# Reordering the seams of a four-deep software pipeline: row statistics, output norm, turned maxima and the residual

## What is computed

```python
def block(x, c):                                   # layers L0, L1, L2, each with its own weights
    s1, c1, g1, s2, c2, g2 = split(silu(c) @ w_mod + b_mod, 6)
    y = layernorm(x) * (1 + c1) + s1
    q, k, v = split(y @ w_qkv + b_qkv, 3)          # 16 heads of 18
    q, k = norm_per_head(q), norm_per_head(k)      # L0: RMS-like, L1: none, L2: centred, with gain and shift
    o = softmax(q @ k.T * 18 ** -0.5) @ v          # per head, 256 x 256
    x = x + g1 * (o @ w_o + b_o)
    y = layernorm(x) * (1 + c2) + s2
    return x + g2 * (gelu(y @ w1 + b1) @ w2 + b2)  # 288 -> 1152 -> 288
U = qr(P).Q                                        # 288 x 64
x = x + ((x @ U) @ expm(A(c)) - x @ U) @ U.T       # after the third block
```

## Time and profile before

| | |
|---|---|
| time, median of 3 runs (lowest to highest) | 5283.6 us (5277.15 to 5285.2) |
| time of the profiled execution | 5279.16 us |
| its span, first to last instruction | 5277.4 us |
| mean granted TensorE clock | 0.942 |
| PE busy | 4467.7 us (85%) |
| DVE busy | 3683.8 us (70%) |
| ACT busy | 2297.4 us (44%) |
| POOL busy | 1110.9 us (21%) |

### The profile page before, as it was taken

How to read it: one execution, slowest core, us unless ns; L and a number is a source line. 1 busy time by engine, 2 the same in 40 slices (tenths; PEclk the granted TensorE clock), 3 DMA queues, 4 the chain that set the end, 5 groups by cost and what they waited for, 6 DMA issues and landing times. The chain is left out here.

```text
span 5277.4 us, 125546 instructions
## 1 busy us (share of the span) xinstructions
PE 4467.7 (85%) x46073; PEld 3701.5 (70%) x46073; DVE 3683.8 (70%) x7723; ACT 2297.4 (44%) x3828; POOL 1110.9 (21%) x2044
## 2 busy tenths in 40 slices
PE   6654888888888886899999999976988989899888
PEld 4543677777777775777777777765777777777776
DVE  5665788777877774666666666656777777777774
ACT  0112445454444543444444444434444444444443
POOL 1001222222222212222222222212122121212121
PEclk7576999999999997999999999997999999999999
DMA  3001010010100001010000100011000000000000
GB/s 69 19 0 47 26 27 27 23 27 21 27 27 24 26 21 55 26 27 25 23 27 27 27 27 27 25 42 31 24 26 19 26 24 21 24 23 26 19 24 17
DMA packets 122230, 141.59 MB, mean 27 GB/s; under 512 B 14446, under 2 KB 117780, under 8 KB 122112
## 3 DMA queue, kind: packets, MB, share of 16 engines
q1 hardware_dynamic: 121968, 139.75, 9.7%
q10 hardware_dynamic: 144, 0.22, 0.0%
HBM read 110.87 MB, written 29.06 MB: 27 GB/s over the span
## 5 line engine op out<-in xcount | busy, mean ns | idle before, releaser
L627 ACT ACTIVATE pT<-S 128x1024 f32<-128x1024 f32 x768 | 745.2, 1022 | 467.5 <-PE S L1134 463.1
L863 DVE TENSOR_REDUCE mx<-S 128x4 f32<-128x1024 f32 x768 | 919.1, 1215 | 26.9 <-PE S L1105 20.0
L575 ACT ACTIVATE hf<-M 128x512 f32<-128x512 f32 (+1 forms) x480 | 266.8, 556 | 927.1 <-PE M L1185 842.7
L922 DVE TENSOR_TENSOR xbo<-M,gM 128x288 f32<-128x288 f32 x192 | 87.8, 457 | 784.1 <-PE M L1224 784.1
L1134 PE MATMUL S<-qT,kT 32*128 32x256 f32 x9216 | 432.2, 298 | 159.3 <-ACT nmT L614 83.7
L504 POOL TENSOR_SCALAR hh<-hf 128x512 fp32r<-128x512 f32 (+1 forms) x480 | 282.7, 589 | 1192.1 <-ACT hf L575 1173.5
L1134 PEld LDWEIGHTS S<-qT,kT 32*128 32x128 f32 x9216 | 336.3, 187 | 240.2 <-ACT pT L627 108.1
L1144 PE MATMUL A<-pT,V 128*32 128x256 f32 x6144 | 415.9, 389 | 19.6 <-ACT pT L627 19.6
L1185 PE MATMUL M<-xh,w_hi 128*128 128x256 f32 x1728 | 388.0, 304 | 4.6 <-POOL xh L480 3.3
L1185 PE MATMUL M<-xl,w_hi 128*128 128x256 f32 x1728 | 347.6, 284 | 40.4 <-DVE xm L786 40.4
L1105 PE MATMUL S<-kT,qT 32*128 32x256 f32 x3072 | 351.2, 337 | 30.9 <-DVE mx L863 24.0
(11 more groups left out here) (229 smaller groups left out, 10190.6 us busy)
## 6 DMA issues: line engine op xcount, KB each, us to landing
mid<-xbo SPq DMA_DIRECT2D x64, 288.0 KB, 3.2
xld<-mid SPq DMA_DIRECT2D x64, 288.0 KB, 3.0
xa<-mid SPq DMA_DIRECT2D x64, 288.0 KB, 3.5
gA<-gates SPq DMA_DIRECT2D x96, 144.0 KB, 3.3
gM<-gates SPq DMA_DIRECT2D x96, 144.0 KB, 3.0
xld<-in_x_dram SPq DMA_DIRECT2D x32, 288.0 KB, 3.5
xa<-in_x_dram SPq DMA_DIRECT2D x32, 288.0 KB, 3.5
out_dram<-xbo SPq DMA_DIRECT2D x32, 288.0 KB, 2.2
```

Source lines behind the costliest of these rows:

```text
L575: act.activation(hf[:, f % 2, 0:c], MBANK[f % 2][:, 0:c], ACT.Gelu if rot else ACT.Gelu_apprx_tanh).then_inc(s["m_hf"], 1)
L627: act.activation(pT[:, g % 2, 2 * h:2 * h + 2, :], S[:, 2 * h:2 * h + 2, :], ACT.Exp, scale=float(HD) ** -0.5).then_inc(s["a_ex"], 1)
L863: dve.tensor_reduce(mx[:, p, :, :], S[:, r:r + 2, :].rearrange("p a (t k) -> p a t k", t=NT), AX.X, ALU.max).then_inc(s["a_mx"], 1)
```

## The change

No operation is added or removed; steps change their places, and one changes its bank.

- DVE: the first half of `M_x2(d)` goes behind both layer norms' statistics and normalisations; `A_heads_norm(p)` goes ahead of the second half of `M_x2(d)`; `R_x3` (third layer) and `A_out(a)` go ahead of `A_lo(p)`; `A_olo` and `M_hl(m, 0)` go ahead of `A_max(p, 1)`; `A_xl(nxt)` goes from ahead of `A_oraw` to a place between `A_max(p, 2)` and `A_x1(a)`.
- PE: `A_turn_max` goes into the previous slot, between `A_qkv(nxt, 4)` and the rest of `down0`, and writes to the fourth score bank, so that it no longer waits for a_qkvd; `A_pv(a, 0)` has that wait now. `down1` is cut at 16 and 22 of its 27 matmuls (first and second layer; before at 9 and 18) and at 16 (third layer; before at 14). `A_turn_n(a)` goes ahead of the scores 0 and 1.
- ACT: `A_shift` goes between the copies of `A_qkv` 4 and 5, in the previous slot.
- POOL: `M_residual` goes behind the first two `M_hh`.

The core of the diff (lines with # name the engine's function):

```diff
 # POOL, slot
-                            M_residual(m)
                             if rot:
                                 M_xh(m)
-                            for f in range(5):
+                            M_hh(m, 0)
+                            M_hh(m, 1)
+                            M_residual(m)
+                            for f in range(2, 5):
                                 M_hh(m, f)
...
 # ACT, A_shift
-                        act.activation(nmT[:, :], ABANK[0][:, 0:T], ACT.Identity).then_inc(s["a_nmc"], 1)
+                        act.activation(nmT[:, :], S[:, 3, 0:T], ACT.Identity).then_inc(s["a_nmc"], 1)
...
 # ACT, slot
-                            A_shift(a)
                             for i in range(2 * QUADS):
...
                             A_qkv(nxt, 4)
+                        if p is not None:
+                            A_shift(p)
+                        if nxt is not None:
                             A_qkv(nxt, 5)
...
 # DVE, slot
-                        if d is not None:
-                            M_x2(d, 0)
                         if m is not None:
                             M_stats(m)
...
                             M_norm(m)
+                        if d is not None:
+                            M_x2(d, 0)
                         if p is not None and eps is not None:
                             A_heads_rstd(p)
+                            A_heads_norm(p, None)
                         if d is not None:
                             M_x2(d, 1)
-                        if p is not None and eps is not None:
-                            A_heads_norm(p, None)
-                        if nxt is not None:
-                            A_xl(nxt)
                         if a is not None:
                             A_oraw(a, 0)
                             A_oraw(a, 1)
+                        if d is not None and rot:
+                            R_x3(d)
                         if m is not None and not rot:
                             M_xl(m)
+                        if a is not None:
+                            A_out(a)
                         if p is not None:
                             A_lo(p, 0)
                             A_lo(p, 1)
-                        if d is not None and rot:
-                            R_x3(d)
-                        if a is not None:
-                            A_out(a)
-                        if p is not None:
                             A_max(p, 0)
                         if m is not None and rot:
                             M_xl(m)
-                        if p is not None:
-                            A_max(p, 1)
-                        if m is not None and not rot:
-                            M_hl(m, 0)
                         if a is not None:
                             A_olo(a)
                         if m is not None:
-                            if rot:
-                                M_hl(m, 0)
+                            M_hl(m, 0)
+                        if p is not None:
+                            A_max(p, 1)
+                        if m is not None:
                             M_hl(m, 1)
                         if p is not None:
                             A_max(p, 2)
+                        if nxt is not None:
+                            A_xl(nxt)
                         if a is not None:
                             A_x1(a)
...
 # PE
-                    def A_turn_max(n, p):
-
-                        if p is not None:
-                            wait(pe, "a_qkvd", p, 6)
-                        wait(pe, "a_prd", n, 0)
+                    def A_turn_max(n):
+
                         wait(pe, "a_nm", n, 1)
                         for t in range(NT):
-                            op = pe.transpose(ABANK[0][:, t * P:(t + 1) * P], nm4[:, t, :, :].rearrange("p r h -> p (r h)"), ident[:, :])
+                            op = pe.transpose(S[:, 3, t * P:(t + 1) * P], nm4[:, t, :, :].rearrange("p r h -> p (r h)"), ident[:, :])
...
-                    def A_pv(n, g):
+                    def A_pv(n, p, g):
...
                         if g == 0:
                             wait(pe, "a_v", n, 2)
+                            wait(pe, "a_prd", n, 0)
+                            if p is not None:
+                                wait(pe, "a_qkvd", p, 6)
...
 # PE, slot
-                            A_turn_max(a, p)
                             A_scoresT(a, 0)
-                            down1(0, 14 if rot else 9)
+                            down1(0, 16)
                             A_scoresT(a, 1)
-                            A_pv(a, 0)
+                            A_pv(a, p, 0)
                             if rot:
-                                down1(14, 27)
+                                down1(16, 27)
...
                             if not rot:
-                                down1(9, 18)
+                                down1(16, 22)
...
                             if not rot:
-                                down1(18, 27)
+                                down1(22, 27)
...
+                        if a is not None:
+                            A_turn_n(a)
                         score(0)
                         score(1)
-                        if a is not None:
-                            A_turn_n(a)
...
                         qkv(4)
+                        if p is not None:
+                            A_turn_max(p)
                         down0(14, 27)
                         qkv(5)
```

More of the change, by code:

```diff
@@ L1299, in slot @@
                             if not rot:
-                                down1(9, 18)
+                                down1(16, 22)
                             A_scoresT(a, 2)
-                            A_pv(a, 1)
+                            A_pv(a, p, 1)
                         if nxt is not None:
@@ L1311, in slot @@
                         if a is not None:
-                            A_pv(a, 2)
+                            A_pv(a, p, 2)
                         if rot and d is not None:
@@ L1317, in slot @@
                         if a is not None:
-                            A_pv(a, 3)
+                            A_pv(a, p, 3)
                         if rot and d is not None:
```

## The result

The changed kernel takes 5538.17 us (median of four runs, 5534.78 to 5542.93) against 5282.79 us; the ratio is 1.0486 (1.0468 to 1.0504). The forecast was 5241.6, at the outside 5312. The profiled execution takes 5534.78 us, its span 5533.1.

A forecast was written before the change was run, and what follows sets the result against it. PE was taken as the bound. Steady slots -51 us, two more slots of each layer -9 and clock +18 summed to -42, giving 5237 profiled, 5241.6 as median; range 5200 to 5275, with the rivals' nearer ends 5150 to 5312.

The forecast's parts named there:

- What bounds the kernel: PE is the bound in all layers, with 4 to 5 us of waits per slot, in three stretches.
- Seam: Last q, k, v matmul to first shifted scores: 2.04 us shrinks to 0.2, transposes cost 0.3 elsewhere; gain 1.5 us.
- Rival 4: Seam doesn't close: negated maxima come late, as `A_xl` is in their chain, and PE waits 0.6 us; 5296 us, chance 0.06.
- Softmax: First shifted scores to last `A_pv`: new `down1` cuts gain 0.65 us per slot in layers 1 and 2, 0.05 in layer 3.
- Back stretch, layers 1 and 2: From V, the last `A_pv`'s start, to scores 5: DVE's chain loses 0.25 us per slot in layer 1, 1.95 in layer 2.
- `A_xl`'s term of 1.15: `A_xl`, moved into DVE's chain between scores 0 and scores 5, adds its whole 1.15 us there.
- the residual's 0.3: POOL's residual, now beside `A_olo` and `M_hl` 0, adds 0.3 us to DVE's chain in layers 1 and 2; bounds 0 and 1.1.
- Rival 1: DVE keeps up, so maximum 3 isn't late for scores 5: about -300 us, 4985 us; chance 0.10.
- rival 3: Residual keeps its price in its new place, holding `M_hl` 0 or 1 by 1.1 us each slot: 5308 us; chance 0.13.
- Back stretch, layer 3: Last `A_pv` to scores 5 in layer 3: V + 24.0 against 22.0, 1.95 us lost per slot.
- Clock: PE's half clock falls in one of four slots of layers 1 and 2, at 1.2 us each: 0.3 us per slot, +18.
- Rival 2: Clock falls in each slot, as 2.6 us idle before scores 5 brings 1.2 GHz: +90 for +18, 5314 us; chance 0.16.

The follow-up runs named there:

- e2: Kernel before with only the seam's part of the change (maxima turned and `A_shift` in the previous slot) and the new `down1` cuts: 5088.04 us, ratio 0.9637.
- e9: e2 with one DVE move added, `A_xl(nxt)` between maximum 2 and `A_x1(a)`: 5157.89 us, ratio 0.9772 to the kernel before.
- e6: e1 with `A_xl(nxt)` back in its old place ahead of `A_oraw` on DVE: 5171.52 us, ratio 0.9802 to the kernel before.
- e7: e2 with POOL's `M_residual` moved behind the first two `M_hh`: 5133.25 us, ratio 0.9731 to the kernel before.
- e1: Changed kernel with 20 (layers 1 and 2) or 15 (layer 3) useless matmuls on PE ahead of scores 5: 5251.60 us, ratio 0.9945 to the kernel before.
- e5: e1 with half the useless matmuls, 10 in layers 1 and 2 and 8 in layer 3: 5291.03 us, ratio 1.0021 to the kernel before.
- e4: Changed kernel with the fifth group of up-projection matmuls ahead of scores 5 in place of behind them: 5325.88 us, ratio 1.0088 to the kernel before.
- e10: e2 with, in layer 3 alone, `R_x3` and `A_out` ahead of `A_lo` and `A_turn_n` ahead of scores 0 and 1: 5132.06 us, ratio 0.9731.
- e12: e2 with the changed DVE and PE order in layers 1 and 2, except `A_xl` ahead of `A_oraw` and maximum 3 between `A_x1`'s halves: 5030.21 us, ratio 0.9533.

## Why the prediction was wrong

**What bounds the kernel** was right: PE, with the waits to be won in three stretches.

**Seam**, -1.5 us a slot, was right: 0.22 us measured for 0.2, the transposes 0.28 with the matmul before them for 0.3, and no wait for the negated maxima. Rival 4 hung on `A_xl` in their chain, which e2 doesn't have; PE's rows of the kernel after, which does, put it out too: the transposes start without a wait, and the shifted scores 0.22 behind the last q, k, v matmul.

```profile
1036.11 0.39 PE L1113 MATMUL S<-ident,nm 128*128 128x128 f32 x2
...
1038.85 0.29 PE L1039 MATMUL A<-wqkv_mix,xm 98*128 98x288 f32 x1
1039.07 0.63 PE L1131 MATMUL S<-qT,kT 32*128 32x256 f32 x12
```

**Softmax**, -0.65, was right: 13.52 us from the first shifted scores to V for the 13.5 forecast. Together the two parts gained 2.12, 2.25 and 1.72 us a slot in e2, for 2.15, 2.15 and 1.55.

**Back stretch, layers 1 and 2**, was right to 0.4 us in each link: maximum 0 at V + 8.3 (8.6), `A_qkv` 0 at V + 16.1 (16.5), its end with the splits, `A_x1` and maximum 3 at V + 19.87 (20.2), scores 5 at V + 19.92 (20.15), idle before it 2.63 (2.6), before `A_qkv` 0 0.61 (0.65). `A_xl`'s term of 1.15 measured 1.16 in layer 2 of e9, and at least 1.02 in e6; the residual's 0.3 measured 0.10 in the kernel after, and `M_hh` 2 held `M_hl` 1 by 0.15 more. In e7's order the same move holds `M_hl` 0 for 0.67, ahead of `A_olo`: what it costs depends on what stands behind the held operation. The Trainium skill, "SBUF — State Buffer", section "SBUF: two separate sides", says that the later of two such operations is blocked until the first ends; e7's rows agree (POOL ends at 1065.53, `M_hl`, which takes 0.68 alone, 0.55 behind it). Without falls a slot takes 44.60 us in e1 for the 44.9 and 45.0 that the sum has ahead of its clock term. Rival 1 is out, and rival 3, a hold of 1.1 us, too.

**Back stretch, layer 3**, was off by 2.0 us: scores 5 at V + 26.0 for V + 24.0. The low products start at V + 12.0 (11.9), but the clock falls there (a pair of matmuls takes 0.80 at 4089.66), and `M_hl` 0 starts at V + 16.0 for 14.8; so 1.2 of the 2.0 lie in the stretch at the lower clock, and belong to the next term. Behind it 10.0 us pass for 9.1: DVE's operations are held by 0.36 us beside the residual, for the 0.5 forecast, and by 0.76 beside `M_hh` 2 and 3 (4097.76 and 4101.00 on POOL), which the sum didn't have. What this order costs without any fall, no run here shows, since each slot with it has one.

**Clock** is the step that failed, in both its factors. It has a fall in one of four slots of layers 1 and 2, at 1.2 us. Measured: 28 of 28; a fall of 3.4 us costs 1.5 (46.08 against 44.6), near the 1.2, but sixteen last 13.7 us, at 5.2 to 5.9 us each (49.8 to 50.5 against 44.6). The sum for the two layers, 60 x 0.3 = 18 us, is 216 (e1: 107 + 109). In layer 3 the term stood at nothing; there 68 us go with the filling alone, and a fall in each slot is still in what remains. Two inferences were at fault. First, that a slot with a gap of 1.81 and a clock of 1.00 speaks for the larger gap: 8 of the 28 slots of that layer have a fall behind the same gaps, so one slot without it says little of the others, and bounds nothing for a larger gap. Second, that a fall lasts as long as the one of the earlier trace rows: its length was taken from a single case, and no upper end set for it. Longer ones stood in the trace of the kernel before, outside the steady slots, as this one of the first slot of layer 1 (columns as in the earlier trace rows):

```profile
537.40:547.60 10.20, 5.75 (x28) 4.96 (x29) 6.02 (x11) 1.67 (x3) 3.27 (x4) 0.50 0.26 73
```

**Rival 2**, a fall in each slot, was the right case, with its reason; its price of 1.2 us, taken from the same row, made it 5314. With the measured 216 for layers 1 and 2 and 68 for layer 3 it would have been about 5223 + 284 = 5507, where 5223 is the sum without a clock term; the rest of the way to 5538 is what remains in layer 3 (in e1 its slots sum to 72 us more than before, 1651.2 against 1579.3, for the 9 of the sum), less 7 us in layers 1 and 2 and less the 24.7 us that lie outside the slots that are summed, for which the sum had nothing. The rule of the Trainium skill that stood beside it ("TensorE: Matmul & The Clock Gate", section "HAM oscillation — how this bites in real kernels"), that a gap which comes back in each tile brings the slow clock back each time, is borne out in layers 1 and 2 of the kernel after (56 of 56 slots), although the page says it of waits for a DMA, longer than those here; it isn't in e5 and e9, where a gap of 1.3 to 1.4 us comes back in each slot and brings the fall in 7 to 11 of 28.

**What stays open.** What decides whether a fall comes, and when in the slot. In the kernel after, 3.4 and 13.7 us follow the same gaps (2.63 and 2.62, each with 0.6 before it), and the length goes with the moment of the fall; that isn't a general rule, since in e4 and e5 falls of 6.8 and 10.2 us begin behind the gap. Which single gap of layer 3 is needed: e10 shows the group, not the member. And how the loss of layer 3 without the clock splits up: the norm-first order (e10, 1.6 us with its fall), `A_xl` (e9, 0.7) and the residual (e7, 0.45) were measured one by one against e2, not together. That the moves on DVE ahead of `A_oraw` (statistics and norms ahead of `M_x2`) cost nothing wasn't tested alone; e12, which has them in layers 1 and 2, is the best version.

## What to carry over

A wait that PE gets in each turn of a tight loop has a second price, the clock of the work behind it, here some 3.5 us a slot (216 over the 62 slots of two layers): look at all gaps that lie close together, not only at the largest, and take the price from the longest fall that a trace shows, not from the nearest one. When a reordering gathers several short waits into a long one, it can lose with no more idle time in sum: in layer 1 PE idles 3.5 us of a slot in the kernel after, in one gap of 2.6 and small ones, and 3.4 in e2, in four of 0.2 to 1.1 behind V, and the slots take 49.8 and 44.7 us. The better orders here keep PE's gaps short and apart. Useless matmuls in the gap are a fast test for this: they add work and leave each engine's order as it is, so what they win back is the clock's.

## What the hardware showed

- After an idle of 2.63 us with 0.61 shortly before it, the granted clock fell to half in 56 of 56 slots; with 1.79 in 28 and 11 of 28, with 1.44 in 9 and 8, with 1.33 in 11 and 7, with 0.25 in none. The number isn't a matter of that gap alone: 1.21 had 21 and 23, and in layer 3 three gaps of 1.05, 0.40 and 0.69 within 4 us gave 28 of 28 (e10), where one of 1.81 gave 8 (before) and 11 (e2).
- The lower clock then held for 3.4, 6.8, 10.2 or 13.7 us, although PE was busy for 13.3 of 13.6 us in such a stretch. In layers 1 and 2 of the kernel after, those that began while PE idled lasted 6.8 or 13.7 (36), those that began with its work again 3.4 (20).
- One fall of 13.7 us costs a slot 5.2 to 5.9 us, less than half of its length, 6.8. One of 3.4 costs 1.5 in the kernel after, and 0.8 in layer 1 of the kernel before (47.54 against 46.78): the price depends on where in the slot it lies.
- A DVE operation on 128 x 512 values with both inputs in SBUF took 1.35 us beside POOL's residual (e7) for 0.68 alone, and ended 0.55 us behind POOL's end.
